# A mixture-of-experts loop on one core: down two tiles behind gate_up, weights split chunk by chunk

## The reference

```python
x = x + xattn(ctx, layernorm(x))            # (4, 512, 512); phase 1, not touched by the change
xn = layernorm(x)                           # 2048 tokens of 512
logits = xn @ router_weight.T + router_bias # 16 experts
top_val, top_idx = top_k(logits, 4); score = softmax(top_val)
for each expert e and each token t that chose it:
    gu = xn[t] @ gate_up_proj[e] + gate_up_bias[e]      # 512 -> 1024, gate and up interleaved
    gate, up = min(gu[::2], 7), clip(gu[1::2], -7, 7)
    h = (up + 1) * gate * sigmoid(1.702 * gate)         # 512
    y = h @ down_proj[e] + down_bias[e]                 # 512 -> 512
    out[t] += score * y
out += x
```

## Time and profile before

| | |
|---|---|
| median of 3 runs | 1053.35 us (1043.41 to 1054.33) |
| span of the profiled execution | 1045.2 us |
| its loop over tiles | from about 290 to 1016 us |
| TensorE busy | 815.1 us, 78% |
| VectorE busy | 619.7 us, 59% |
| ScalarE busy | 405.9 us, 39% |
| instruction packets (queue q14) | 100, 0.82 MB |

### The profile page before, as it was taken

How to read it: one execution, slowest core, us unless ns; L and a number is a source line. 1 busy time by engine, 2 the same in 40 slices (tenths; PEclk the granted TensorE clock), 3 DMA queues, 4 the chain that set the end, 5 groups by cost and what they waited for, 6 DMA issues and landing times.

```text
span 1045.2 us, 17727 instructions
## 1 busy us (share of the span) xinstructions
PE 815.1 (78%) x3572; PEld 640.2 (61%) x3573; DVE 619.7 (59%) x1066; ACT 405.9 (39%) x659; POOL 336.3 (32%) x379
## 2 busy tenths in 40 slices
PE   5238164455289999988998989889889989899981
PEld 2034142424068877877876867777778777787771
DVE  3786577564746564656747557567557465665450
ACT  4974765702033332433424324334424243342220
POOL 1550724851613232322322223223233232332220
PEclk9556565555589999999999999989999999999995
DMA  8210123131117372457546264565556363633236
GB/s 297 83 41 0 41 41 121 41 97 45 48 35 202 63 202 42 103 143 200 149 96 198 43 196 127 122 182 139 158 148 186 57 149 94 187 57 61 45 58 181
DMA packets 69035, 116.99 MB, mean 112 GB/s; under 512 B 27616, under 2 KB 29920, under 8 KB 68864
## 3 DMA queue, kind: packets, MB, share of 16 engines
q1 hardware_dynamic: 29280, 77.55, 20.7%
q0 software_dynamic: 18336, 38.35, 20.0%
q10 hardware_dynamic: 21312, 0.16, 1.2%
HBM read 87.91 MB, written 32.31 MB: 115 GB/s over the span
## 4 chain that ended last, share of the span: by engine, by line
PE 56%; DVE 12%; issue 10%; DMA 6%; ACT 6%; POOL 4%; ACTq 3%; DVEq 1%; SPq 0%; POOLq 0%
PE gate_up_ps L737 25%; PE bank L737 20%; DMA acc_rows<-yb,aslot 3%; PE bank L719 2%; POOL slot_rows L342 2%; PE bank L727 2%; ACT junk L458 2%; DMA xg<-xn_rows,gslot 2%; PE gate_up_ps L709 2%; DVE hl L1097 1%; DVE work L861 1%; ACTq L233 1%; PE gate_up_ps L641 1%; ACTq L529 1%; DVE work L856 1%
## 5 line engine op out<-in xcount | busy, mean ns | idle before, releaser
L737 PE MATMUL gate_up_ps<-w,xh 128*128 x1152 | 364.7, 398 | 1.7 <-DVE xl L1092 1.7
L386 POOL DMA_INDIRECT acc_rows<-yb,aslot x72 | 133.8, 1858 | 502.5 <-ACT yb L556 496.0
L737 PEld LDWEIGHTS gate_up_ps<-w,xh 128*128 128x128 f32 x1152 | 213.1, 190 | 43.6 <-issue 2.1
L737 PE MATMUL bank<-w,hh 128*128 x576 | 192.6, 417 | 44.9 <-DVE hl L1097 44.8
L737 PE MATMUL gate_up_ps<-w,xl 128*128 x576 | 226.3, 393 | 0.0
L1097 DVE TENSOR_TENSOR hl<-bank,hh 128x512 fp32r<-128x512 f32 x72 | 49.6, 689 | 191.5 <-ACT hh L543 191.5
L737 PEld LDWEIGHTS bank<-w,hh 128*128 128x128 f32 x576 | 113.6, 200 | 78.3 <-issue 55.0
L543 ACT CAST hh<-bank 128x512 fp32r<-128x512 f32 x72 | 42.3, 587 | 229.5 <-PE bank L727 127.3
L737 PEld LDWEIGHTS gate_up_ps<-w,xl 128*128 128x128 f32 x576 | 108.8, 189 | 24.1
L1103 DVE TENSOR_TENSOR gu<-gate_up_ps,bgu 128x1024 f32<-128x1024 f32 x72 | 88.1, 1223 | 56.4 <-PE gate_up_ps L737 56.4
L1128 DVE TENSOR_TENSOR w<-raw_w,w 128x1536 f32 x60 | 102.9, 1756 | 28.8 <-issue 17.7
(11 more groups left out here) (190 smaller groups left out, 836.7 us busy)
## 6 DMA issues: line engine op xcount, KB each, us to landing
raw_w<-_L_ffn_gate_up_proj_dram SPq DMA_DIRECT2D x32, 1024.0 KB
raw_w<-in_L_ffn_down_proj_dram SPq DMA_DIRECT2D x32, 512.0 KB
bgu<-n_gate_up_proj_bias_dram SPq DMA_DIRECT2D x16, 512.0 KB
x_sb<-in_x_dram SPq DMA_DIRECT2D x4, 1024.0 KB, 10.6
xn_rows<-xn SPq DMA_DIRECT2D x4, 1024.0 KB, 4.5
acc_rows<-x SPq DMA_DIRECT2D x4, 1024.0 KB
gslot<-slot_rows ACTq DMA_DIRECT2D x75, 1.0 KB, 3.6
xg<-xn_rows,gslot POOLq DMA_INDIRECT x74, 4.4
```

What stands on the lines that cost most here:

```text
L386: pool.indirect_dma_start(acc_d, bass.IndirectOffsetOnAxis(aslot[:, k, 0:1], 0), yb[:, k % 2, :], None, compute_op=ALU.add).then_inc(S["ad ...
L737: last = nc.tensor.matmul(out_ps, lhs[:, rows], w[:, bass.ds(buf, 1), part, c, cols].rearrange("p a d -> p (a d)"), start=(m == 0), stop=( ...
```

## The change

- PE's step: both halves of gate_up with the transposes of x between them, then down of tile T-2, then the transposes of h of tile T-1. After the loop: down, transposes, down.
- ACT and DVE make hh and hl of tile T-2 in step T, and ACT scales y of tile T-2.
- The gather runs three tiles ahead, gslot is loaded four tiles ahead, aslot for tile T itself at the end of step T, and the add of tile T-3 is made in step T.
- The split goes by chunk: chunk 0 at the end of an expert's second step, chunk 1 behind hh and chunk 2 behind xh in its third, chunk 3 behind hh in its fourth. An expert of three tiles splits chunks 0 and 1 at the end of its second step and 2 and 3 in its third. There are five tests a step on ACT (three of them behind y) where there were four, and five on DVE where there were two. Chunk number and buffer are register values.
- At least two tiles an expert (LEAST), a fourth bias slot (so SP's loop goes by four experts and not by three), junk laid into that slot during phase 1, scratch of the table moved to sim, and a shorter chain of small VectorE steps that build the table.

```diff
-TILES = -(-(TOKENS * TOP_K // P + E - 1) // UNROLL) * UNROLL
+LEAST = 2
+TILES = -(-(TOKENS * TOP_K // P + LEAST * E) // UNROLL) * UNROLL
...
-        bgu = sb("bgu", [P, 3, GU])
+        bgu = sb("bgu", [P, 4, GU])
...
-        junk = sb("junk", [P, RT, N], mybir.dt.bfloat16)
+        junk = bgu[:, 3, :].bitcast(mybir.dt.bfloat16).rearrange("p (r n) -> p r n", r=RT)
...
@@ GpSimd's step @@
-                gather(T + 2, (k + 2) % UNROLL)
-                if not known(T):
-                    add(T - 1, (k - 1) % UNROLL)
+                gather(T + 3, (k + 3) % UNROLL)
+                if not known(T, 3):
+                    add(T - 3, (k - 3) % UNROLL)
...
@@ ScalarE @@
+            def high_w(buf, c):
+                where = buf * (2 * HC) + c
+                nc.scalar.copy(w_v[:, where, :] if isinstance(where, int) else w_v[:, bass.ds(where, 1), :].rearrange("p a d -> p (a d)"),
+                               raw_w[:, c, :] if isinstance(c, int) else raw_w[:, bass.ds(c, 1), :].rearrange("p a d -> p (a d)")).then_inc(S["hi_done"], 1)
+
+            def split_now(own, name):
+
+                with act.If(field(act, own, name)):
+                    buf, c = 1 - field(act, own, "buffer"), field(act, own, "chunk")
+                    high_w(buf, c if name == "early" else after(act, c))
+
+            def split_late(own):
+
+                for name, chunks in (("late_0", (0,)), ("late_1", (1,)), ("late_23", (2, 3))):
+                    with act.If(field(act, own, name)):
                         buf = 1 - field(act, own, "buffer")
...
+                        if name == "late_0":
+                            act.wait_ge(S["raw_in0"], 48 * field(act, own, "expert") + 96)
+                            act.wait_ge(S["raw_in1"], 32 * field(act, own, "expert") + 64)
+                        for c in chunks:
+                            high_w(buf, c)
...
-                load_slots(field(act, offs, "slots_3"), (k + 3) % UNROLL, gslot, gslot_in)
-                if not known(T):
-                    high_h(T - 1, (k - 1) % UNROLL)
+                load_slots(field(act, offs, "slots_4"), k, gslot, gslot_in)
+                if not known(T, 2):
+                    high_h(T - 2, (k - 2) % UNROLL)
+                    split_now(own, "early")
                 high_x(T + 1, (k + 1) % UNROLL)
-                split_high(own, "early")
+                if not known(T, 2):
+                    split_now(own, "mid")
                 sigmoid(T, k)
-                if not known(T):
-                    scale_y(T - 1, (k - 1) % UNROLL)
-                split_high(own, "late")
-                if not known(T, 3):
-                    act.wait_ge(S["added"], 16 * (T - 2))
-                load_slots(field(act, offs, "slots_1"), (k + 1) % UNROLL, aslot, aslot_in)
+                if not known(T, 2):
+                    scale_y(T - 2, (k - 2) % UNROLL)
+                if not known(T, 4):
+                    act.wait_ge(S["added"], 16 * (T - 3))
+                load_slots(field(act, offs, "slots_0"), k, aslot, aslot_in)
+                if not known(T, 1):
+                    split_late(own)
...
@@ TensorE's step @@
                 gate_up(T, k, 0, buf)
+                tr_x(T + 1, (k + 1) % UNROLL)
+                gate_up(T, k, 1, buf)
+                if not known(T, 2):
+                    down(T - 2, (k - 2) % UNROLL, field(pe, own, "buffer_before"))
                 if not known(T):
                     tr_h(T - 1, (k - 1) % UNROLL)
-                tr_x(T + 1, (k + 1) % UNROLL)
-                gate_up(T, k, 1, buf)
-                if not known(T):
-                    down(T - 1, (k - 1) % UNROLL, field(pe, own, "buffer_before"))
...
@@ VectorE's step @@
-                if not known(T):
-                    low_h(T - 1, (k - 1) % UNROLL)
+                if not known(T, 2):
+                    low_h(T - 2, (k - 2) % UNROLL)
+                    split_now(own, "early")
                 low_x(T + 1, (k + 1) % UNROLL)
+                if not known(T, 2):
+                    split_now(own, "mid")
                 gate(T, k, field(dve, own, "bias"))
-                split_low(own)
+                if not known(T, 1):
+                    split_late(own)
```

More of the change, by code:

```diff
@@ L31 @@
 WIDE = GU + H
-TABLE = TILES + 4
+TABLE = TILES + 5
 LAPS = TILES // UNROLL
[L39 to L42, removed]
+FIELDS = {"expert": (0, 4, E - 1), "buffer": (0, 1, 1), "bias": (0, 2, 3), "late_0": (4, 1, 1), "late_1": (5, 1, 1),
+          "late_23": (6, 1, 1), "early": (7, 1, 1), "mid": (8, 1, 1), "chunk": (9, 2, HC - 1), "buffer_before": (11, 1, 1),
+          "slots_0": (0, 9, SLOTS // P), "slots_4": (9, 9, SLOTS // P)}
 HALF = HC // 2
@@ L237, in field, with after @@
             return nc.s_assert_within(eng.snap((value >> at_bit) & ((1 << bits) - 1)), 0, most,
+                                      skip_runtime_bounds_check_because="the table is built within these bounds")
+        def after(eng, chunk):
+            return nc.s_assert_within(eng.snap(chunk + 1), 1, HC - 1,
                                       skip_runtime_bounds_check_because="the table is built within these bounds")
@@ L293, in _ @@
                     sp.wait_ge(S["lo_done"], HC * (e - 1) + HALF * (h + 1))
[L294 to L296 removed]
+                    load_half(e, h, e)
+            with sp.Fori(1, E // 4) as four:
+                for j in range(4):
                     for h in range(2):
[L298 to L299 removed]
+                        sp.wait_ge(S["lo_done"], HC * 4 * four + (HC * (j - 1) + HALF * (h + 1)))
+                        load_half(4 * four + j, h, j)
             sp.wait_ge(S["all_added"], 1)
@@ L1051, in _ @@
-            link(V.tensor_tensor(tabs(5), ttab[:, 0:TABLE - 1], tabs(1), ALU.subtract))
-            steps = slice(0, TABLE - 3)
-            last, last_1, last_2 = (tf[:, 4, i:TABLE - 3 + i] for i in range(3))
-            nth, splits, early, spare = tf[:, 5, steps], tf[:, 6, steps], tf[:, 7, steps], word_f[:, 0, steps]
-            link(V.memset(tabs(6), 0.0))
-            link(V.tensor_tensor(splits, last, last_1, ALU.max))
-            link(V.scalar_tensor_tensor(out=splits, in0=splits, scalar=3.0, in1=last_2, op0=ALU.mult, op1=ALU.max))
@@ L1080, in _ @@
-            link(V.tensor_copy(word_f[:, 1, TABLE - 3:TABLE], tf[:, 3, 0:3]))
+            steps = slice(0, TABLE - 2)
+            expert, first = tf[:, 0, steps], tf[:, 1, steps]
+            nth, ends, ends_2, flags = (tf[:, row, steps] for row in (2, 4, 5, 6))
+            link(V.tensor_tensor(nth, ttab[:, steps], first, ALU.subtract))
+            link(V.tensor_tensor(ends, tf[:, 0, 1:TABLE - 1], expert, ALU.subtract))
+            link(V.tensor_tensor(ends_2, tf[:, 0, 2:TABLE], expert, ALU.subtract))
@@ new lines, in _ @@
+            link(V.tensor_tensor(word_f[:, 0, steps], flags, expert, ALU.add))
+            link(V.tensor_copy(word_f[:, 0, TABLE - 2:TABLE], tf[:, 0, TABLE - 2:TABLE]))
+            link(V.scalar_tensor_tensor(out=word_f[:, 0, 2:TABLE], in0=tf[:, 0, 0:TABLE - 2],
+                                        scalar=float(1 << FIELDS["buffer_before"][0]), in1=word_f[:, 0, 2:TABLE],
+                                        op0=ALU.mult, op1=ALU.add))
+            link(V.tensor_scalar(tf[:, 3, :], tf[:, 3, :], 1.0 / P, None, ALU.mult))
@@ L1132, in step, with split_now, split_late @@
+            def split_now(own, name):
+                with dve.If(field(dve, own, name)):
+                    c = field(dve, own, "chunk")
+                    low_w(own, c if name == "early" else after(dve, c))
+            def split_late(own):
+                for name, chunks in (("late_0", (0,)), ("late_1", (1,)), ("late_23", (2, 3))):
+                    with dve.If(field(dve, own, name)):
+                        for c in chunks:
+                            low_w(own, c)
             def step(T, k):
```

106 lines of the change are left out of this document (43 added, 63 removed).

## The result

The changed kernel takes 1133.85 us (median of 4 runs, 1130.41 to 1135.9) against 1053.84: a ratio of 1.080, interval 1.074 to 1.086. It is slower, as forecast, but by 80 us and not 49, and 1134 lies above the range of 1057 to 1125.

What follows compares the result with a forecast made beforehand. It took ScalarE's instruction fetch at sixteen loop jumps, delaying down on TensorE, to bound the kernel. Terms summed to +49.4 us, chiefly code +28.8 and clock +10, on 1053.35: 1103 us, range 1057 to 1125.

Steps and rivals of the forecast that it cites:

- What bounded the kernel: TensorE's loop: sixteen waits of down for hl at loop jumps, because ScalarE must fetch instructions; all waits for hl 43.1 us.
- It still touches four blocks, and so still misses its first.: ScalarE's changed loop, counted as 306 instructions from 566, was to miss its first code block at each jump.
- At experts of four and more tiles ... No wait.: VectorE's weight splits: gate ends at 12.2 us, transposes of h want it at 17.7, so no wait.
- Three-tile experts, forecast +2.6: Weight splits at the five experts of three tiles: 1.6 us each against 1.06 before, +2.6 us.
- Code, +28.8: ScalarE at the sixteen jumps: second code block wanted ahead of gslot and hh, 1.8 us each, +28.8 (11 to 45).
- Third test, +0.29 each: ScalarE after y: three tests instead of two, the untaken one 0.29 us, 16 times, +4.6 us.
- Clock, +10: TensorE's granted clock drops after longer waits at jumps: 0.6 us times 16, +10 us (0 to 20).
- Start and tail, +1.0: Start of the loop gains 1.6 us, the extra down at the end costs 2.6; both +1.0 us.
- A clean step "so 9.08": TensorE's undisturbed step keeps the same 44 products and transposes, so stays at 9.08 us.
- VectorE's loop: Grows from 208 to some 338 instructions and may touch four blocks; its miss ends 2 us ahead of hh, costing nothing.
- The Trainium skill's blocks of 16 KiB: Rule of 256-instruction blocks, two kept: ScalarE's loop of 306 would fit, giving 993 us, not 1103; forecast held the trace disagrees.
- ACT's loop fits: Rival, chance 0.15: ScalarE's loop fits its kept code blocks, the sixteen waits at jumps go, 993 us.

Runs made afterwards that it cites:

- run 3: Kernel before with 31 instructions of padding (already met waits) ahead of ScalarE's loop, so it touches three code blocks: 988.3 us, ratio 0.941.
- 4: Changed kernel with ScalarE scaling y ahead of the sigmoid, same number of instructions: 1142.44 us, ratio 1.090.
- 5: Kernel of run 1 with VectorE making gate ahead of the early and mid weight splits: 1059.74 us, ratio 1.014.
- 9: Kernel of run 1 with only the mid weight split moved behind gate on VectorE: 1059.29 us, ratio 1.009.
- 13: Changed kernel, chunks 1 and 2 split behind gate only in the third tile of longer experts, by a flag; three blocks on both engines: 1021.66 us, ratio 0.972.
- run 1: Changed kernel with 13 instructions of padding ahead of ScalarE's loop, so it touches three code blocks: 1051.97 us, ratio 1.0015.
- run 7: Kernel before with 18 waits ahead of ScalarE's loop: still four blocks, the second wanted at the 14th instruction, not the 32nd: 1067.99 us, ratio 1.024.
- 10: Changed kernel with the order of work of before, new splits, gathers and loads kept, 9 waits of padding, three blocks: 1046.54 us, ratio 0.998.
- 12: Kernel of 9 with the transposes of h ahead of down instead of behind it: 1061.76 us, ratio 1.011.
- run 8: Kernel of 5 with 45 waits ahead of VectorE's loop, so that loop touches four blocks by one instruction: 1118.14 us, ratio 1.069.
- 2: Changed kernel with 12 instructions of padding ahead of ScalarE's loop, one fewer than run 1, so it touches four blocks: 1160.42 us, ratio 1.104.

## Why the prediction was wrong

Without the misses the change costs 64 us (988.3 to 1052.0), and with them 80 to 84 (1133.85 against 1053.84, or against the 1050.2 of the later runs): the misses of code cost the kernel before 62 us (1050.2 to 988.3) and the changed one 82 (1133.85 to 1051.97). So they account for 20 of the difference. The forecast had it the other way, nearly all of its 49 in code at the jumps and the low clock behind.

- **What bounded the kernel.** Right, and shown by run 3: sixteen jumps, ScalarE's instruction fetch, 62 us. The order of work on PE had no part in it: with the loop in three blocks and nothing else changed they go.
- **"It still touches four blocks, and so still misses its first."** Right; the hand count was off by 3 and 8 instructions, with 13 to the edge.
- **"At experts of four and more tiles ... No wait."** This is the step that failed. The working had gate delayed and asked only whether the transposes of h would be late for it. They are not. But ScalarE takes its work in order: the sigmoid needs gate, and behind it stand y, aslot, the jump, and hh of the next step. A gate 3 us late is an hh 3 us late. The front of the document has that order in its list of ScalarE's step. Without misses this costs 1.8 to 2.5 us of wait and mostly a slow down product at each longer expert; with a jump right behind, lateness and miss add up to 7 us. Both the place and the cause are shown: y first didn't help (4), and moving the splits behind gate took waits for hl away (5, 9, 13), for the price of others where chunk 3 was moved as well. Where it wasn't (13), the kernel gained 30 of the 64 us. The forecast put 0 here.
- **Three-tile experts, forecast +2.6.** Right in kind, mis-sized: in the first run five times 3.5 us, over two steps, with a wait of 1.3 to 1.5 for hl in the first of them; before it was 1.2 us. So +11.5.
- **Code, +28.8.** The second block's pause is real, but was priced too high: 0.7 us a jump in run 7, where I asked for it alone, and not 1.8, and +18.6 with the low clock, for which the sum had another 10. In the changed kernel's trace it is 0.7 to 1.3 us at eight of the fourteen jumps that can be read, and 0.3 at the others. The first miss itself is no dearer than before, 2.4 to 5.6 us in both kernels. It costs more because less of it is hidden: before, hh came 56 us later over the sixteen jumps than in run 3, and 39 us of that became waits for hl; in the changed kernel it came 69 us later than in run 1, and the waits grew by 64.
- **Third test, +0.29 each.** It fits, though no run tried it alone: y to gslot in a clean step was 2.67 us and is 2.98:

```profile
908.62 0.69 ACT L562 ACTIVATE yb<-bank,aslot 128x512 f32<-128x512 f32 x1 [0.32 <-PE bank L758]
...
911.60 0.34 ACTq L535 DMA_DIRECT2D gslot<-slot_rows  x1
```

- **Clock, +10.** Right in kind, and near: what follows the waits at jumps, mostly low clock, grew by 15.7 us. The waits themselves grew by 45, where the terms for code and tests had 35.
- **Start and tail, +1.0.** Some +10: the first two steps of the loop cost 3.6 us more than before, with 3.0 of waits for hl and xl in them, and some 6.8 remain for the tail, whose last two down products wait 3.6 and 1.8 (before one, 1.8).
- **A clean step "so 9.08".** 9.15, +4.9 in all, and it goes with transposes of h that stand apart from those of x (runs 10 and 12). Why that costs 0.07 stays open.
- **Gather.** Right, its waits on PE are gone.
- **VectorE's loop.** "Its miss would end 2 us ahead of hh": it did not come to that, since 316 instructions from 984 fit three blocks; run 8 says that this step of the forecast would have been wrong, by 58 us.
- **The Trainium skill's blocks of 16 KiB**, two kept ("Runtime: NRT & Kernel Launch", section "Instruction fetch mechanics"). Its other half, that a taken branch out of the kept window must fetch, is what all runs show. Its block size does not fit, if blocks lie alike in both kernels: with 256 instructions a block and two kept, before (673 to 1009) misses and run 3 (704 to 1040) does not, only if a block begins somewhere from 674 to 704, and runs 1 and 2 differ only if one begins at 576, and so at 832. These are no multiple of 256 apart. Blocks of 128 that begin at 576, 704 and so on, with a miss where four are touched, give before, the changed kernel and runs 1, 2, 3, 5, 7 and 8.

The rival "ACT's loop fits" (993) did not come about, and run 1 says that its price would have been wrong as well: 1052, as the late gate stays.

## To carry to other kernels

When a producer moves back in an in-order queue, follow everything that stands behind its consumer in the consumer's queue, into the next step and over the loop's jump, and not only the one reader that the data was for. When a hardware loop's waits repeat with its number of written-out steps, look for instruction packets in the loop, count the blocks of the code it touches on each engine, and try a few instructions of padding ahead of it; on ScalarE that moved these kernels by 62 to 108 us. And when two edits of a schedule cancel, look whether one flag serves two cases: the same place in the code was harmless for experts of one length and late for the other.

## What the hardware showed that I had not expected

- One more instruction ahead of the loop, 1160.4 to 1052.0 us: whether the jump misses goes by whole blocks, for ScalarE (1 against 2, 3 against before) and for VectorE (8 against 5, +58 us).
- A miss at the jump stops ScalarE for 2.4 to 2.6 us where the DMA engines are busy for a third of that time or less, and for 4.0 to 5.6 us where they are busy for 90% or more of it, as when weights are loaded (before and the changed kernel). Where the loop begins one instruction ahead of a block (2), a second pause of 2.0 to 3.4 us follows.
- Waits that are already met cost little as padding: in run 3 they start 0.075 us apart, 2.3 us for the 31 instructions, once and ahead of the loop, and the kernel is 62 us faster.
